# Output projection in two passes: 16 heads plain, 16 heads as seven block products by pairs of token tiles

## What is computed

```python
out = jnp.einsum('bhqk,bkhd->bqhd', attn, v).reshape(B, S, H * VD)
return out @ wo.T
...
x = x + _L1_attn_ref(_layernorm(x, axis=-1), ...)
x = x + _L1_ffn_ref(_layernorm(x, axis=-1), ...)
```

## Time and profile before

| | us |
|---|---|
| median of 3 runs (1580.81 to 1582.98) | 1580.95 |
| profiled execution | 1582.47 |
| its span, first to last instruction | 1580.7 |
| TensorE busy | 1520.3 |
| VectorE busy | 1092.3 |
| ScalarE busy | 898.3 |
| GpSimd busy | 857.7 |

### The profile page before, as it was taken

The page is one execution under the profiler, slowest core; times in us unless marked ns, Lnnn a source line. Parts: engine busy times, 40 slices in busy tenths (PEclk is TensorE's granted clock), DMA queues, the critical chain, the costliest instruction groups (busy, mean ns, idle before and its releaser), DMA issues. The chain is left out here.

```text
span 1580.7 us, 32072 instructions
## 1 busy us (share of the span) xinstructions
PE 1520.3 (96%) x12288; PEld 926.7 (59%) x12288; DVE 1092.3 (69%) x2791; ACT 898.3 (57%) x1680; POOL 857.7 (54%) x754
## 2 busy tenths in 40 slices
PE   5998999999989999999999999999999999999999
PEld 4655555555556777777767777654444444445554
DVE  8898859986778888888888888853412210177784
ACT  6877323323769999999999999962211100022221
POOL 4223245445948888888888888850122210056652
PEclk9999999999999999999999999999999999999999
DMA  9894245554947999999999999987966781375555
GB/s 369 297 335 169 67 94 139 145 157 107 170 98 135 187 188 186 186 191 192 199 188 185 189 177 188 193 179 220 237 186 145 179 223 27 97 177 134 106 127 141
DMA packets 611577, 272.91 MB, mean 173 GB/s; under 512 B 532704, under 2 KB 579936, under 8 KB 611296
## 3 DMA queue, kind: packets, MB, share of 16 engines
q1 hardware_dynamic: 611424, 270.86, 74.2%
HBM read 81.54 MB, written 56.10 MB: 87 GB/s over the span
## 5 line engine op out<-in xcount | busy, mean ns | idle before, releaser
L2396 POOL TENSOR_TENSOR xb<-xb 128x1280 f16<-128x1280 f32 x128 | 335.7, 2623 | 6.8 <-ACT xb L2299 6.8
L2291 ACT ACTIVATE xb<-bk,D_sv,qw_c 128x512 f32<-128x512 f32 (+3 forms) x512 | 289.1, 623 | 2.6 <-DVE D_sv L2354 2.5
L2345 DVE TENSOR_REDUCE bk<-bk 128x1 f32<-128x512 f32 (+3 forms) x512 | 227.6, 490 | 16.5 <-PE bk L2241 15.7
L2299 ACT ACTIVATE xb<-xb 128x1280 f16<-128x1280 f32 x128 | 162.6, 1271 | 13.6 <-DMA xb<-xb 9.9
L2256 PE MATMUL D_t<-vh,xb 128*128 128x65 f16 x1280 | 130.8, 194 | 1.6 <-DVE D_on L2364 1.6
L2257 PE MATMUL D_t<-vl,xb 128*128 128x65 f16 x1280 | 130.9, 192 | 0.0
L2258 PE MATMUL D_t<-vh,xb 128*128 128x65 f16 x1280 | 130.3, 193 | 0.0
L2256 PEld LDWEIGHTS D_t<-vh,xb 128*128 128x128 f16 x1280 | 118.7, 97 | 2.5 <-issue 2.2
L2257 PEld LDWEIGHTS D_t<-vl,xb 128*128 128x128 f16 x1280 | 118.5, 98 | 0.4
L2258 PEld LDWEIGHTS D_t<-vh,xb 128*128 128x128 f16 x1280 | 118.6, 97 | 0.0
L92 POOL TENSOR_SCALAR mv<-mv 128x1 f32<-128x1 f32 x64 | 22.2, 346 | 147.2 <-DVE mv L87 146.0
(11 more groups left out here) (454 smaller groups left out, 4672.4 us busy)
## 6 DMA issues: line engine op xcount, KB each, us to landing
od<-D_os SPq DMA_DIRECT2D x32, 512.0 KB, 4.5
xd<-xb SPq DMA_DIRECT2D x16, 512.0 KB, 4.0
ow_raw<-mwd SPq DMA_DIRECT2D x32, 256.0 KB, 3.4
xb<-xd SPq DMA_DIRECT2D x16, 512.0 KB, 6.2
ow_raw<-in_w SPq DMA_DIRECT2D x32, 256.0 KB, 4.2
out_x<-xb SPq DMA_DIRECT2D x32, 256.0 KB, 3.0
w1d<-xb SPq DMA_DIRECT2D x16, 448.0 KB, 4.5
xb<-in_x SPq DMA_DIRECT2D x6, 1024.0 KB, 14.1
```

The costliest lines, as they stand in the source:

```text
L2291: m = e.activation(p[:, AT[i]:AT[i] + N], Sb[n % 4][:, c:c + N], ACT.Exp, scale=qw.col(qw.NEG, g), bias=s[:, 7 - i:8 - i])
L2299: e.activation(P2[u % 3][:, 0:1280], P[u % 3][:, :], ACT.Copy).then_inc(s_ph, 1)
L2345: m = e.tensor_reduce(minima(u, i), Sb[n % 4][:, c:c + N], AX.X, ALU.min)
L2396: e.tensor_tensor(P2[u % 3][:, 1280:2560], P[u % 3][:, :], P2[u % 3][:, 0:1280], ALU.subtract).then_inc(s_pl, 1)
```

## The change

What it does:

- The first eight chunks of the fused matrix (heads 0 to 15) are multiplied as before, tile by tile, 48 matmuls a tile. Then a second pass makes the other eight chunks by pairs of tiles with seven block products (`PRODUCTS`, `GOES`, `read_before`, now shared with the last layer): per pair 7 x 4 chunks x 3 matmuls, added to `xb` by seven DVE reads.
- `FusedBlocks` prepares the seven blocks of the second half of the matrix in eight pieces: two loads, four sums on POOL, four high parts on ACT, four low parts on DVE, and a store of three of the blocks, which are loaded again during tile 15. Two output buffers.
- `PairSums` makes the four operand sums of a pair from the turned float16 parts on DVE (8 operations of 128 x 512), the high parts on ACT, the low parts on POOL.
- `od` is turned in halves of 16 blocks, each half tile when its pass needs it. In the attention six pieces are turned ahead, not nine.
- The squares of the last weights stand between the pieces on ACT (`SQUARES`), in two buffers of their own; `TOTALS` is 6; the items of the last weights come after tiles 7 to 11 and have two output buffers. Nothing lies in `xb` any more.
- The last layer's first pair is prepared in the last pair of the second pass (it was after tiles 0 and 2); all seven of its blocks are loaded there, the i-th after product i.
- Sums on DVE that were `tensor_tensor` are `scalar_tensor_tensor` with a factor of 1.0.
- POOL clears the semaphores of a finished stage at the start of the next, in three more places.

The diff, cut:

```diff
@@ OutWeights
-    EARLY = 6
+    EARLY, PLAIN = 6, 8
+        self.slots = [sb(f"ot{i}", [128, 16, 128]) for i in range(6)]
...
@@ FusedBlocks (new)
+    def sp_load(self, e, w, n):
+        j, c = self.PIECES[n]
+        if n < 3:
+            w.wait_ge(self.ow.s_ml, 6 + n)
+        else:
+            w.wait_ge(self.s_lo, n - 2)
...
+    def act_high(self, e, w, n):
+        self.landed(w, n)
+        w.wait_ge(self.s_sums, 4 * n + 4)
+        w.wait_ge(self.s_out[n % 2], 32 * (n // 2))
...
@@ PairSums (new)
+    def act_high(self, e, w, p, i):
+        w.wait_ge(self.s_sum, 8 * p + (8 if i else 6))
+        w.wait_ge(self.s_p, 7 * (p - 2) + (7 if i else 5))
+        e.activation(self.made(p, i)[:, 0, :], self.sums[i], ACT.Copy).then_inc(self.s_hi, 1)
...
@@ LastWeights.sp_load_squared
-        w.wait_ge(self.s_sq, q - 2)
+        w.wait_ge(self.s_sq, q - 1)
...
@@ PairFeed.dve_sums (one of four)
-            e.tensor_tensor(sa[:, lo], h2[:, lo], h2[:, hi], ALU.add).then_inc(self.s_sum, 1)
+            e.scalar_tensor_tensor(sa[:, lo], h2[:, lo], 1.0, h2[:, hi], ALU.mult, ALU.add).then_inc(self.s_sum, 1)
...
@@ attention, sp
-            for p in range(3):
+            for p in range(2):
...
@@ out_projection
-    TOTALS = 5
-    LOWS = {6: (0, 1, 2), 7: (3, 4, 5), 8: (6, 7, 8, 9, 10)}
+    TOTALS = 6
+    LOWS = {2: [("m", 0), ("m", 1), ("m", 2)], 3: [("m", 3), ("m", 4)], 4: [("m", 5), ("m", 6)], 5: [("m", 7)],
+            7: [("l", 0), ("l", 1)], 8: [("l", 2), ("l", 3)], 9: [("l", 4), ("l", 5)], 10: [("l", 6), ("l", 7)],
+            11: [("l", 8), ("l", 9), ("l", 10)]}
+    SQUARES = {0: (0,), 1: (1,), 2: (2,), 3: (3, 4), 4: (5,), 5: (6, 7), 6: (8,), 7: (9, 10)}
...
+        def block_product(p, i):
+            _, kind, k0, blk = PRODUCTS[i]
+            W = mb.pe_block(w, blk)
+            ps.pe_made(w, p, kind)
+            w.wait_ge(ps.s_fin, read_before(p, i))
+            for k in range(4):
+                x = mm3(e, bank(p, i)[:, :], ps.operand(p, kind, k0 + k), (W[0][:, k, :], W[1][:, k, :]), ...)
+            x.then_inc(ps.s_p, 1)
...
@@ out_projection, act
+        for n in range(8):
+            mb.act_high(e, w, n)
+            for q in SQUARES[n]:
+                lx.act_square(e, w, q)
+        for n in range(len(lx.ITEMS)):
+            lx.act_high(e, w, n)
+        for p in range(NP):
+            for i in range(2):
+                ps.act_high(e, w, p, i)
         for v in range(4):
             pf.act_high(e, w, v)
...
@@ out_projection, dve
+        for p in range(NP):
+            if p == 2:
+                for q in range(3):
+                    stats(q)
+            if p == NP - 1:
+                w.wait_ge(ps.s_p, 7 * p)
+                for q in range(2):
+                    pf.dve_apply(e, w, q, xb)
+            for i in range(7):
+                read(p, i)
+                if p + 1 < NP and i < 4:
+                    ps.dve_sums(e, w, p + 1, (2 * i, 2 * i + 1))
+                if p == NP - 1 and i < 2:
+                    pf.dve_sums(e, w, 0, i)
+                if p == NP - 1 and i == 2:
+                    stats(3)
...
@@ out_projection, pool
+        for p in range(NP):
+            for i in range(2):
+                ps.pool_low(e, w, p, i)
...
+        for v in range(4):
+            pf.pool_low(e, w, v)
+        norm.pool_rstd(e, w, N_F1 + 3)
         for q in range(2):
             lx.pool_bias(e, w, norm, q, xb[:, pf.tile(q), :])
...
@@ out_projection, sp
+        for j in range(4, NT):
+            w.wait_ge(s_col, j - 3)
+            ow.sp_turn(e, j % 4, j, 0)
...
+            for kind, n in LOWS.get(j - 3, ()):
+                if kind == "m":
+                    mb.sp_store(e, w, n)
+                    if n + 3 < 8:
+                        mb.sp_load(e, w, n + 3)
+                    elif n >= 5:
+                        lx.sp_load(e, w, n - 5)
+                    for q in SQUARES[n]:
+                        for r in [next(squares, None)]:
+                            if r is not None:
+                                lx.sp_load_squared(e, w, r)
...
+        for n in range(4, NT):
+            turn_pair(n)
+        for i in range(7):
+            w.wait_ge(ps.s_p, 7 * (NP - 1) + i + 1)
             lx.sp_load_block(e, w, i)
+            if i in (2, 4, 5):
+                pf.sp_turn(e, w, {2: 0, 4: 1, 5: 2}[i])
@@ lora_layer1, sp
         pf.sp_turn(e, w, 3)
-        for i in range(4, 7):
-            lx.sp_load_block(e, w, i)
```

More of the change, by code:

```diff
@@ L258, in layers @@
         g["ow"] = ow = OutWeights(nc, root, mwd, od, ms)
-        g["lx"] = lx = LastWeights(nc, root, a)
-        g["pf"] = pf = PairFeed(nc, root, norm)
+        g["s_result"] = root.enter_context(nc.semaphore("result"))
         mid, banks = ExitStack(), ExitStack()
@@ L283, in layers @@
                 g["wa"] = SmallWeights(nc, right, a["wa"], keep)
-                lora_layer0(spent=ph, **g)
+                p0 = lora_layer0(spent=ph, **g)
                 ph.release()
+            g["lx"] = lx = LastWeights(nc, root, a)
+            g["pf"] = pf = PairFeed(nc, root, norm)
+            g["mb"] = mb = FusedBlocks(nc, root, ow)
+            g["ps"] = ps = PairSums(nc, root)
             ow.place_weights(root)
@@ L344, in sem @@
         def sem(what):
-            return ctx.enter_context(nc.semaphore(f"wa_{what}"))
+            return nc.alloc_semaphore(f"wa_{what}")
         self.src = src.rearrange("(k p) n -> p k n", p=128)
@@ L829, in splits @@
         x, c = self.ITEMS[n]
-        raw = self.raw[(self.N + n) % 3]
+        raw = self.raw[self.slot(n)]
         if x == "g":
@@ L1943, in lora_layer0, with projections @@
     ph.ctx.close()
-def projections(nc, a, wbs, s_wb, s_xd, cst, half, ident, xb, qT, kT, v, norm, feed, wa, ow, bk, qu, **_):
+    return ph
+def projections(nc, spent, a, wbs, s_wb, s_xd, cst, half, ident, xb, qT, kT, v, norm, feed, wa, ow, bk, qu, **_):
     ph = Scope(nc, "C")
@@ L2123, in rstd_qk @@
             e.tensor_tensor(s[:, 4:6], s[:, 2:4], half.to_broadcast([128, 2]), ALU.pow).then_inc(s_rq, 1)
+        spent.pool_clear(e)
         e.memset(v[0][:, :, 64:65], 1.0)
@@ L2158, in projections, with attention @@
     ph.ctx.close()
-def attention(nc, wbs, od, s_wb, s_ot, cst, ident, xb, kT, v, qw, ow, qu, **_):
+    return ph
+def attention(nc, spent, wbs, od, s_wb, s_ot, cst, ident, xb, kT, v, qw, ow, qu, **_):
     NU = 128
@@ L2447, in sp @@
                         ow.sp_turn_piece(e, j, p)
-        for kt in range(ow.EARLY + 1, ow.EARLY + 3):
-            ow.sp_load(e, w, kt)
+        ow.sp_load(e, w, 7)
     with nc.Block() as block:
@@ L2489, in pe @@
         for j in range(G):
-            for kt in range(12, 16):
+            for kt in range(EARLY, PLAIN):
                 product(j, kt)
         for j in range(G, NT):
-            for kt in range(16):
+            for kt in range(PLAIN):
                 product(j, kt)
@@ L2518, in add, with read @@
                 e.scalar_tensor_tensor(dst, ob[2 * (j % 3) + hf][:, :], ms.col(ms.INV), dst, ALU.mult, ALU.add).then_inc(s_add, 1)
+        def read(p, i):
+            q, c = GOES[i]
+            t = pf.tile(2 * p + q)
+            dst = xb[:, t, 512 * c:512 * c + 512]
+            w.wait_ge(s_add, 2 * t + 2)
+            w.wait_ge(ps.s_p, 7 * p + i + 1)
+            if i in (1, 4, 5):
+                w.wait_ge(ps.s_fin, 7 * p + {1: 1, 4: 4, 5: 3}[i])
+            e.scalar_tensor_tensor(dst, bank(p, i)[:, :], ms.col(ms.INV), dst, ALU.mult, ALU.add).then_inc(ps.s_fin, 1)
         def stats(q):
-            w.wait_ge(s_add, 2 * pf.tile(q) + 2)
+            w.wait_ge(ps.s_fin, 7 * (q // 2) + 7)
             pf.dve_stats(e, w, q, xb)
-        for kt in range(EARLY, 16):
+        for kt in range(EARLY, PLAIN):
             ow.dve_low(e, w, kt)
@@ L2565, in load_x, with turn_pair @@
             e.dma_start(xb[:, t, :], xd[t, :, :]).then_inc(s_x[t // 4 % 2], 16)
-        loads = iter(range(EARLY + 3, 16))
+        def turn_pair(n):
+            p, i = divmod(n, 2)
+            s = ps.slot(p, i)
+            if p == 0:
+                w.wait_ge(s_col, 13 + i)
+            elif p == 1:
+                w.wait_ge(lx.s_lo, 8)
+            else:
+                w.wait_ge(ps.s_p, 7 * (p - 2) + (6 if i else 2))
+                w.wait_ge(ps.s_sum, 8 * (p - 2) + 8)
+            ow.sp_turn(e, s, pf.tile(n), 1)
```

410 lines of the change are left out of this document (272 added, 138 removed).

## The result

The changed kernel takes 1594.06 us (median of 4 runs, 1592.25 to 1596.5), the kernel before beside it 1580.88: ratio 1.0083, 95% interval 1.007 to 1.0096. It is 13 us slower, where 5.7 were forecast; the time lies inside the range. The profiled execution has a span of 1593.1 us against 1580.7, so 12.4 us have to be found. Both are single executions.

The account below looks back on a forecast made before the run. The output projection was taken as bound by TensorE's matmuls alone; -20.8 + 14 + 0.9 + 13 - 3.5 - 1.3 + 3.4 = +5.7 us against the median 1580.95 gave 1586.7 us, range 1572 to 1596.

Parts of the forecast that it names:

- Matmuls removed: Output projection: 1440 matmuls instead of 1536, 96 at 0.2166 us each, -20.8 us as long as nothing stalls TensorE.
- Preparation beside the first pass: Behind tile 6 TensorE waits for the last weights' squares; DMA work ends the last at 1131, tile 7 14 us late.
- Second pass: Pairs of tiles in the output projection: DVE keeps pace, only statistics ahead of pair 2 delay a read, +0.9 us.
- End of the stage: Meeting of engines after the output projection: turn 1 behind block loads makes POOL late, +13 us (bounds +7.3 and +18).
- Gates of pair 1: Last layer: two waits for turns queued behind the weights' loads go, -3.5 us (0 if POOL's later start keeps them).
- Attention: Three of nine early turns leave the attention, where ScalarE waited behind two of them: -1.3 us (0 to -1.4).
- The clock: Two new long TensorE gaps each followed by about 3.4 us at half clock: +3.4 us (0 to 4).
- (a): The forecast itself, both waits (totals and end of the output projection): 1584 to 1592 us, chance 0.48.
- (d): SP itself is held in its turns and everything behind slips in both places: 8 us more, 1595 us, chance 0.12.
- (b): Totals behind tile 6 never wait, pieces come at 4.7 us, +1 for +14: 1572 us, chance of faster 0.22.
- (c): At the end of the output projection turn 1 isn't caught behind the weights: 5.7 us less, 1581 us, chance 0.15.
- (e): Second pass: products save nothing, POOL holds DVE's reads and sums, which pace pairs at 20.8 us: 1607 us, chance 0.03.

Follow-up runs that it names:

- the experiment above: Kernel before, with three of nine early turns and one of two last chunk loads moved from the attention to the output projection's start: 1581.41 us, ratio 1.0.
- totals: Changed kernel with the totals taken behind tile 8 instead of tile 6, items of the last weights behind tiles 8 to 12: 1585.81 us, ratio 1.0036.
- biases behind the sums: Against totals behind tile 8, early POOL biases and early SP turns together, POOL waits for the pair's four sums before the biases: 1575.24 us, ratio 0.9973.
- turn 2: Against the version whose POOL biases wait for the pair's four sums, SP's turn 2 moves to the start of the last layer: 1579.03 us, ratio 0.9979.
- all three edits: Changed kernel with totals behind tile 8, POOL's bias additions early and SP's turns ahead of the block loads: 1577.78 us, ratio 0.9986.

## Why the prediction was right, and where its sizes were off

The mechanism was right: 96 fewer matmuls, two new waits at the forecast places, for the forecast reasons. The size was not: 13 us where 5.7 were forecast.

- **Matmuls removed, -20.8.** Right: 96 fewer. That they would be spent on two waits, and on which, is what happened.
- **Preparation beside the first pass, +14.** Right in mechanism and place, too small: the wait at the totals is 16.6 us where about 11 were forecast, and the idle times of the stage up to there come to 19.9. I forecast the last square at 1131 and it ended at 1132.4, but by luck of two errors: the stage began 5 us earlier than I assumed, and the chain took 73.6 us from the first matmul where I had 67.3 (1131 less 1063.7). TensorE was at the totals at 1115.9. The mis-sized step is the sum of DMA work: from 1060 to 1132 the queues moved 20.7 MB at a mean of 288 GB/s, with a share of 0.94 to 1.17 in every 10 us. That is about the work I had listed (18.0 MB and five half turns, which are 2.6 MB), but it took 72 us and not 62.7. The packets of this window, summed from the trace's records by size:

| packet | MB | us of all queues | us a MB | in the sum |
|---|---|---|---|---|
| 256 B (turns) | 3.02 | 19.9 | 6.6 | 5.0 |
| 512 and 544 B | 3.31 | 11.6 | 3.5 | 2.76 |
| 1 KB | 5.24 | 17.4 | 3.3 | 2.76 |
| 2 KB | 4.90 | 14.5 | 3.0 | 2.76 |
| 4 KB | 4.19 | 11.4 | 2.7 | 2.76 |

Together they are 74.8 us, 1.04 times the window, as its share says. So the price that I read from 4 KB packets holds for these alone. My sentence "I count short rows of pieces like long ones from no row of their own" names one weak place, worth about 6 us; the other, about as large, is the turns: one alone cost 5.2 us for 1.05 MB, and among other work 256 B packets cost a third more. That the last square is late by the sum and not by SP's holds was not separated: SP's hold of 7.67 us delayed the first store by 6.0 us, and ScalarE waited 8.38 for it.
- **The form of the sums frees nothing.** Shown.
- **Second pass.** Blocks at 2.6 us, and a wait of 0.60 us ahead of pair 2 for the statistics, forecast +0.9; another 0.24 stands in the last pair.
- **End of the stage, +13.** It is +15.7. The chain is the one forecast, link by link: turn 1, high 3, low 3, root, biases. I had turn 1 landed at T+24.3; the last pair starts at T = 1356.5, and high 3 began at 1383.58, T+27.1. From there to the first gates it took 9.0 us, as forecast (9.1). The 2.8 us are SP's: held for 6.98 us in turn 0, it issued the fourth load at 1372.29 where I had it at T+10.4, and turn 1 at 1374.33 where I had T+13. I had kept this for the upper bound (18), as what a held issue can cost, and should have put it in the sum: all six profiles with this order of SP's list have 6.20 to 6.98 us there.
- **Gates of pair 1, -3.5.** Right: both waits (1.87 and 1.61) are gone.
- **Attention, -1.3.** About right, by the experiment above: 1.2 in one pair of profiles. The start is 5.0 earlier in the profile, most of it not by the forecast mechanism.
- **The clock, +3.4.** Too low: 5.0. Behind the totals 12 matmuls stand 0.43 us apart instead of 0.22 (2.6 us), and behind the end of the stage the gates lose 2.4. TensorE's windows (busy, granted clock, DMA share, GB/s) show 1.2 instead of 2.4 GHz at the end of the first wait and behind both:

```profile
1130.00:1132.00 2.00, 0.00 (x0) 0.50 1.12 191
...
1134.00:1136.00 2.00, 2.00 (x6) 0.50 1.01 340
1136.00:1138.00 2.00, 2.00 (x6) 0.50 0.93 303
1138.00:1140.00 2.00, 2.00 (x10) 0.93 1.01 337
...
1394.00:1396.00 2.00, 2.00 (x21) 0.50 1.26 47
```

- **Rivals.** The waits are those of (a), but 1594.06 lies above its 1584 to 1592; that the range holds it is owed to (d). (b), the totals never wait, is out. (d), SP held in its turns, named what was missing at the end of the stage, shows in the first pass too, and its 1595 was the nearer number. (c) and (e) didn't happen: turn 1 was caught, and DVE kept pace.

## What to carry to other kernels

When a change halves the time of a stage that hid a preparation, sum the DMA work that has to be through by each point, and price it from packets of the sizes that those transfers have, turns among them; the matmuls saved are worth only what this sum leaves free. Look at what stands last before a meeting of all engines: an order in which the turns come ahead of big loads gained about 8 us here without touching any work, and a held transpose on the engine that issues the DMAs delays everything behind it. A wait that goes uncovers the next one. Here a third of it came back (totals), more than half (biases behind the sums) or all of it (turn 2).

## What the runs showed of the hardware that was not expected

A transpose directly behind loads held SP for long in these traces: 6.98, 7.11 and 4.85 us at the end of the stage behind three, two and one block loads of 1 MB, 8.32 us behind three of them in another version, against a median of 1.95 in the earlier trace rows. Directly behind another transpose it was 1.85 us. Why is not shown.

TensorE's clock fell behind single gaps among running matmuls, not only behind the two long ones. Behind idle times of 3.73 and 3.98 us (the turns of tile 7) and 3.75 us (the late read) the next matmul took 0.59 to 0.61 us, the granted clock read 0.50 in the windows behind, and 2.6 to 2.9 us were lost; behind 2.12 us at tile 6 of the changed kernel, and behind 3.28 in the version with all three edits, it took 0.38 and the clock stayed at 1.00. The gaps of the first kind so cost about 1.7 times their own length.
